# Node transposes moved behind the edge transposes and into the bank of the node sums

## The chip, the cores and the metric

One core of a Trainium2 chip runs the whole program. The metric is the device time of one execution in microseconds (us), as the median of several executions. Engines are named as in the profile: PE is TensorE's matmul, PEld its weight load, DVE is VectorE, ACT is ScalarE, POOL is GpSimd, SP is SyncE, which issues DMAs.

## What is computed

A graph layer over 50,000 nodes and 50,000 edges, 128 features each, in float32. `h` is the layer norm of `x` with negatives set to zero. Every edge takes its source's row of `h`, scales it by its weight, multiplies it with the 128x128 matrix of its type (one of 32) and is added to its destination. Every node also gets `h @ loop_weight + bias`. The matrices of the types are mixtures of 8 bases.

```python
h = jnp.maximum(_layernorm(x, axis=-1), 0.0)
W_rel = jnp.einsum('rb,bdf->rdf', w_comp, weight)
agg = jax.ops.segment_sum(h[src] * norm, seg, num_segments=n_rels * n_nodes)
node_repr = jnp.einsum('rnd,rdf->nf', agg.reshape(n_rels, n_nodes, d_in), W_rel)
out = x + jax.nn.relu(node_repr + h_bias + h @ loop_weight)
```

The edges come sorted by destination.

## The kernel before, in words

**Tiling.** Edges go in 98 groups (NG) of G = 4 tiles of 128 edges, nodes in 98 groups (NGW) of 4 windows of 128 nodes. One step `g` works on both at once, each part with its own lag, and there are 104 steps. Every engine has its own program, unrolled over the steps, in a hand-written order; engines meet only through semaphores. An engine takes its instructions strictly in order, so a wait holds up all that stands behind it.

**Edge side of step g.** POOL gathers rows of `x`. ACT subtracts means and applies relu (`normalised`, L685), PE transposes the four tiles of `h` into the PSUM bank `hT_ps` (L900), ACT copies the bank to `hT` (L719). In the next step PE multiplies each tile j with all eight bases: `messages(j)` is `product_high` (L813, bases 4 to 7) and `product_low` (L820, bases 0 to 3), each a 128x512 product which the trace shows as two matmul records. ACT scales three of the eight results (`scale_bases`: `z` L622 from the high product, then two `z` L626 from the low one), POOL adds two of them (`u` L526), and DVE adds the other five with the type's weights (L1075) and makes `msg` (L1108). I call DVE's block for one tile a slot: `tile_slot(j)`, which begins with the sum that reads the `z` of L622. Five PSUM banks `y_ps` take the products in rotation, so `product_high` of a tile waits until DVE has ended `sum_a` of three tiles before (L812), `product_low` until `sum_b` of two tiles before.

**Node side.** With lag 2 DVE takes statistics of `xw`. With lag 4 (RELU_AT) ACT makes `hw` for four windows (`window_relu`, L664, one after each of its four mixing blocks). With lag 5 (TURN_AT) PE transposes `hw` into `hT_ps` (`window_transposes`, L826), ACT copies that to `hwT` (`window_hT`, L673), and DVE makes the one-hot rows `pick` (`window_rows`, L1182). With lag 6 (SUMS_AT) PE multiplies `hwT` with the loop weight into the bank `win_ps` (`window_self`, L830), adds the messages to it with `pick` (`window_sums`, L835), and DVE reads the sums, applies relu and adds `x` (`window_results`, L1195). SP stores `res`.

**Order of PE in a step.** messages(0), messages(1), the node transposes of group g-5, the self products and sums of group g-6, messages(2), the small product for the type weights (L891), the four edge transposes, messages(3). Node and edge transposes share `hT_ps`, so the edge transposes wait for ACT's copy of the node ones (L898).

**Order of ACT in a step.** mixing(0), two normalised tiles, three square roots, window(0), mixing(1), two normalised tiles, the copy L673, window(1), mixing(2), the copy L719, window(2), two sums for means, mixing(3), two sums of squares, window(3).

**Order of DVE in a step.** slot 0, slot 1, the reciprocal and means, `window_rows`, `window_results`, slot 2, the type weights, slot 3, hot rows, shift and means of nodes. Each slot 0 and 1 ends with statistics of one edge tile and one window.

```python
messages(0)
messages(1)
if node_group(g, TURN_AT) is not None:
    window_transposes(g - TURN_AT)
...
pe.wait_ge(s_relu, g * G + G)
if node_group(g, TURN_AT) is not None:
    pe.wait_ge(n_hT_sb, g - TURN_AT + 1)
for j in range(G):
    mm = nc.tensor.transpose(hT_ps[:, j, :], h[:, q, j, :], ident[:, :])
mm.then_inc(s_hT, 1)
```

Of the kernel before, what the change touches and what calls it, by code (L numbers as in the profile page):

```python
# [20 lines left out]
ACT = mybir.ActivationFunctionType  # L21
# [17 lines left out]
HRING = 2  # L39
# [9 lines left out]
TURN_AT = 5  # L49
SUMS_AT = 6  # L50
# [29 lines left out]
def round_after(n, q, ring=RING):  # L80

    return n + (q + 1) // ring

def beyond(g, n):

    return isinstance(g, int) and g >= n

def is_before(g, n):  # L90

    return isinstance(g, int) and g < n
# [12 lines left out]
def build_layer(nc, x, src, dst_cols, dst, dst_next, type_rows, norm, dst_far, weight, mix_weight, loop_weight, bias, out):  # L105
    N, D = x.shape
    NT = src.shape[1]
    NG = NT // G
# [10 lines left out]
    STEPS = NGW + SUMS_AT  # L119
# [12 lines left out]
    with ctx:  # L132
        def sb(name, shape, dt=F32):
            return ctx.enter_context(nc.sbuf_tensor(name, shape, dt))

        def psum(name, shape, dt=F32):
            return ctx.enter_context(nc.psum_tensor(name, shape, dt))

        def sem(name):
            return ctx.enter_context(nc.semaphore(name))  # L140
# [6 lines left out]
        ident = sb("ident", [P, P])  # L147
# [75 lines left out]
        hw = sb("hw", [P, HRING, G, D])  # L223
        hwT = sb("hwT", [P, HRING, G, P])
# [16 lines left out]
        win_ps = psum("win_ps", [P, G, F])  # L241
        hT_ps = psum("hT_ps", [P, G, P])
# [8 lines left out]
        def late_bank(i):  # L251

            return y_ps[(2 * NG * G + i) % 5]

        def win_of(k):

            return win_ps if k < NGW - LATE else late_bank(k - (NGW - LATE))
# [25 lines left out]
        s_meta = sem("s_meta")  # L283
# [74 lines left out]
        n_hT_sb = sem("n_hT_sb")  # L358
        n_y = sem("n_y")
        n_res = sem("n_res")  # L360
# [6 lines left out]
        def node_group(g, at):  # L367

            return g - at if 0 <= g - at < NGW else None

        def windows_of(k):

            return G if k < NGW - 1 else LAST_FULL + 1
# [240 lines left out]
        def _(act):  # L614
# [54 lines left out]
            def window_hT(k):  # L669
                act.wait_ge(n_hT, k + 1)  # L670
                if k >= HRING:
                    act.wait_ge(n_y, k - (HRING - 1))
                nc.scalar.activation(hwT[:, k % HRING, :, :], hT_ps[:, :, :], ACT.Copy).then_inc(n_hT_sb, 1)  # L673

            def step(g, n, q):
                here = g < NG

                def mixing(j):
                    if 1 <= g <= NG:
                        scale_bases(g - 1, (q - 1) % RING, j)  # L680

                def normalised(tiles):

                    for j in tiles:
                        nc.scalar.activation(h[:, q, j, :], xg[:, q, j, :], ACT.Relu,  # L685
                                             bias=neg_mean[:, q, j:j + 1]).then_inc(s_relu, 1)

                def window(j):
                    k = node_group(g, RELU_AT)
                    if k is not None and j < windows_of(k):  # L690
                        window_relu(k, j)

                mixing(0)
                if here:
                    act.wait_ge(s_mean, g + 1)
                    act.wait_ge(s_squares, g * (G - DV))
                    if not is_before(g, RING):
                        act.wait_ge(s_hT, g - (RING - 1))
                    normalised(range(0, G // 2))
                    if not is_before(g, RING):  # L700
                        act.wait_ge(s_rstd, g - (RING - 1))
                    nc.scalar.activation(std[:, q, 0:DV], mv[:, q, :, 1], ACT.Sqrt, bias=eps_col[:, 0:1])
                    nc.scalar.activation(std[:, q, DV:G], squares[:, q, :], ACT.Sqrt, bias=eps_col[:, 0:1],
                                         scale=1.0 / D).then_inc(s_std, 1)
                if node_group(g, STD_AT) is not None:
                    window_std(g - STD_AT)
                window(0)
                mixing(1)
                if here:
                    normalised(range(G // 2, G))  # L710
                if node_group(g, TURN_AT) is not None:
                    window_hT(g - TURN_AT)
                window(1)
                mixing(2)
                if here:
                    act.wait_ge(s_hT, g + 1)
                    if not is_before(g, RING):
                        act.wait_ge(s_y, g * G - (RING - 1) * G)
                    nc.scalar.activation(hT[:, q, :, :], hT_ps[:, :, :], ACT.Copy).then_inc(s_hT_sb, 1)  # L719
                window(2)  # L720
                if not beyond(g, NG - 1):
                    group_means(g + 1, round_after(n, q), (q + 1) % RING)
                mixing(3)
                if not beyond(g, NG - 1):
                    group_squares(g + 1, (q + 1) % RING)
                window(3)
# [43 lines left out]

            first_step()
            sweep(act, STEPS, step, first=2)

            act.wait_ge(s_table, 16)
# [17 lines left out]
        def _(pe):  # L792
# [29 lines left out]

            def window_transposes(k):
                pe.wait_ge(n_h, k + 1)
                for j in range(windows_of(k)):
                    mm = nc.tensor.transpose(hT_ps[:, j, :], hw[:, k % HRING, j, :], ident[:, :])  # L826
                mm.then_inc(n_hT, 1)

            def self_loop(bank, v, j):
# [32 lines left out]
            def step(g, n, q):  # L862
                def messages(j):
                    if 1 <= g <= NG and not (is_before(g, 2) and j < PAIR):
                        if j == (PAIR if is_before(g, 2) else 0):
                            pe.wait_ge(s_hT_sb, g)
                        product_high(g - 1, (q - 1) % RING, j)
                        product_low(g - 1, (q - 1) % RING, j)

                messages(0)  # L870
                messages(1)
                if node_group(g, TURN_AT) is not None:
                    window_transposes(g - TURN_AT)
                if node_group(g, SUMS_AT) is not None:
                    for j in range(G):
                        window_self(g - SUMS_AT, j)
                if node_group(g, SUMS_AT) is not None and g != STEPS - 2:
                    if g == STEPS - 1:
                        window_sums(NGW - 2)
                    window_sums(g - SUMS_AT)  # L880
                messages(2)
                if is_before(g, 2):
                    messages(3)
                if g < NG:
                    pe.wait_ge(s_hot, g + 1)
                    if not is_before(g, 1):
                        pe.wait_ge(s_mix, g)
                    if g == CROWD_STEP:
                        pe.wait_ge(s_crowded, 1)
                        nc.tensor.matmul(mix_ps[0:1, 0:1], ones16[:, :], crowded16[:, :], start=True, stop=True)  # L890
                    nc.tensor.matmul(mix_ps[:, P:P + G * B], hotT[:, q, :], w_mix[:, :],  # L891
                                     start=True, stop=True).then_inc(s_mix_ps, 1)
                    if is_before(g, 1):
                        first_tiles()
                        return
                    pe.wait_ge(s_relu, g * G + G)
                    if node_group(g, TURN_AT) is not None:
                        pe.wait_ge(n_hT_sb, g - TURN_AT + 1)  # L898
                    for j in range(G):
                        mm = nc.tensor.transpose(hT_ps[:, j, :], h[:, q, j, :], ident[:, :])  # L900
                    mm.then_inc(s_hT, 1)
                if not is_before(g, 2):
                    messages(3)

# [23 lines left out]
            with pe.If(compact > 0):  # L928
# [8 lines left out]
                with pe.Fori(0, NGW) as g:  # L937
                    pe.wait_ge(f_h, g + 1)
                    hold(pe, passed["pe"])
                    for j in range(G):  # L940
                        mm = nc.tensor.transpose(hT_ps[:, j, :], hw[:, 0, j, :], ident[:, :])
# [10 lines left out]
        def _(dve):  # L952
# [245 lines left out]
            def window_results(k):  # L1198
                r = k % NRING
                dve.wait_ge(n_y, k + 1)  # L1200
                if k >= NRING:
                    dve.wait_ge(n_out[r], 16 * (k // NRING))
                results(win_of(k), r, k % XRING, windows_of(k)).then_inc(n_res, 1)

            def step(g, n, q):
                more, here = not beyond(g, NG - 1), not beyond(g, NG)
# [16 lines left out]
                    means(g + 1, (q + 1) % RING)  # L1223
                if g == STEPS - 3:
                    window_results(g - SUMS_AT)
                if node_group(g, TURN_AT) is not None:
                    window_rows(g - TURN_AT)
                if node_group(g, SUMS_AT) is not None and g != STEPS - 3:
                    window_results(g - SUMS_AT)
                tile_slot(g, n, q, 2, False)  # L1230
                stats_of(2)
# [205 lines left out]
```

## Time and profile before

| what | value |
|---|---|
| median of 3 runs | 1015.7 us (1014.95 to 1016.97) |
| the profiled execution, its own time | 1014.06 us |
| its span, first to last instruction | 1012.3 us |
| busy: PE, DVE, ACT, POOL | 995.7, 946.5, 882.8, 723.9 us |
| mean granted clock of TensorE | 0.995 of full speed |
| DMA | 154.46 MB, 153 GB/s mean |

A timeline lists instructions of one engine in order of time: start in us from the span's start, duration, engine, line, operation, tiles written and read, shape, count of merged instructions, and in brackets the idle time before and who ended it. Records of one engine overlap, since its instructions are pipelined, so the time that an instruction takes of its engine is read from start to start, not from its duration. The waits view gives the total, the number and the longest.

### The profile page before, as it was taken

Reading aid. Unit: us, or ns where it says so; the run is one execution under the profiler, and the core shown is the slowest. Engines: PE = TensorE matmul, PEld = TensorE weight load, DVE = VectorE, ACT = ScalarE, POOL = GpSimd, SP = SyncE. Lnnn points to the kernel's source line nnn. Section 1 sums busy time; section 2 is a strip of 40 time slices with the busy share of each in tenths; the row PEclk is TensorE's granted clock in tenths of the full one; section 3 lists DMA queues with packets and bytes.
Section 4 is the critical chain, followed back from the end, with each engine's and each line's share of the span. In section 5 each row is a group of like instructions: output and inputs, shape, how many; then the busy total and the mean of one; then the engine's idle time right before and its main releaser. Section 6 shows DMA issues by size and latency. Waiting matters only on the chain.

```text
span 1012.3 us, 23603 instructions
## 1 busy us (share of the span) xinstructions
PE 995.7 (98%) x4912; PEld 578.3 (57%) x4912; DVE 946.5 (94%) x4372; ACT 882.8 (87%) x3237; POOL 723.9 (72%) x1183
## 2 busy tenths in 40 slices
PE   7999999999999999999999999999999999999996
PEld 3455655555656565655555555556565555565655
DVE  8899999999999999999999999999999999999995
ACT  6798988889898989898989898989888888989884
POOL 7887767777777777777777777777776777777740
PEclk9999999999999999999999999999999999999999
DMA  4556556555556565565565565565655655655544
GB/s 116 148 143 169 154 145 167 147 156 158 151 147 176 137 164 158 152 164 158 138 175 139 157 162 155 147 170 148 165 155 141 173 141 157 158 159 139 154 124 138
DMA packets 178222, 154.46 MB, mean 153 GB/s; under 512 B 17781, under 2 KB 151213, under 8 KB 178077
## 3 DMA queue, kind: packets, MB, share of 16 engines
q1 hardware_dynamic: 157261, 101.40, 36.0%
q0 software_dynamic: 20384, 51.32, 20.7%
q14 instruction: 105, 0.86, 0.3%
q8 instruction: 40, 0.66, 0.3%
q10 hardware_dynamic: 432, 0.22, 0.1%
HBM read 101.31 MB, written 51.56 MB: 151 GB/s over the span
## 4 chain that ended last, share of the span: by engine, by line
PE 95%; ACT 2%; DVE 1%; POOL 1%; DMA 1%; issue 1%; ACTq 0%; DVEq 0%; POOLq 0%
PE y_ps L813 34%; PE y_ps L820 32%; PE win_ps L835 9%; PE win_ps L830 8%; PE hT_ps L900 4%; PE hT_ps L826 4%; PE mix_ps L891 1%; POOL xg L573 0%; DMA xg<-x,src_all 0%; ACT z L626 0%; ACT hw L664 0%; PE y_ps L835 0%; DMA src_all<-src 0%; PE y_ps L830 0%; DVE sum_a L1075 0%
## 5 line engine op out<-in xcount | busy, mean ns | idle before, releaser
L573 POOL DMA_INDIRECT xg<-x,src_all x392 | 386.6, 986 | 65.1 <-issue 48.6
L813 PE MATMUL y_ps<-w_all,hT 128*128 128x512 f32 x784 | 412.9, 608 | 3.3 <-DVE sum_a L1075 2.2
L820 PE MATMUL y_ps<-w_all,hT 128*128 128x512 f32 x784 | 401.9, 594 | 0.0
L526 POOL TENSOR_TENSOR u<-z 128x128 f32<-128x128 f32 x392 | 180.9, 461 | 189.5 <-ACT z L626 186.0
L626 ACT ACTIVATE z<-y_ps,mix 128x128 f32<-128x128 f32 x784 | 244.8, 367 | 45.3 <-PE y_ps L820 45.2
L1075 DVE SCALAR_TENSOR_TENSOR sum_b<-y_ps,mix,sum_b 128x128 f32<-128x128 f32 x784 | 266.4, 340 | 0.1
L820 PEld LDWEIGHTS y_ps<-w_all,hT 128*128 128x128 f32 x784 | 149.5, 191 | 188.6 <-issue 148.3
L813 PEld LDWEIGHTS y_ps<-w_all,hT 128*128 128x128 f32 x784 | 133.2, 190 | 118.0 <-DVE sum_a L1075 61.3
L622 ACT ACTIVATE z<-y_ps,mix 128x128 f32<-128x128 f32 x392 | 141.0, 360 | 62.6 <-PE y_ps L813 61.6
L664 ACT ACTIVATE hw<-xw,shift,nrstd 128x128 f32<-128x128 f32 x391 | 192.8, 494 | 0.4 <-DVE shift L1177 0.4
L1075 DVE SCALAR_TENSOR_TENSOR sum_b<-y_ps,mix,z 128x128 f32<-128x128 f32 x392 | 133.1, 339 | 47.7 <-ACT z L622 47.4
L1075 DVE SCALAR_TENSOR_TENSOR sum_a<-y_ps,mix,u 128x128 f32<-128x128 f32 x392 | 133.8, 341 | 2.9 <-POOL u L526 2.9
L685 ACT ACTIVATE h<-xg,neg_mean 128x128 f32<-128x128 f32 x384 | 135.1, 413 | 0.0
L1075 DVE SCALAR_TENSOR_TENSOR sum_a<-y_ps,mix,sum_a 128x128 f32<-128x128 f32 x392 | 134.0, 342 | 0.3 <-DVE sum_b L1075 0.2
L1108 DVE TENSOR_TENSOR msg<-sum_a,sum_b 128x128 f32<-128x128 f32 x392 | 113.7, 290 | 0.1
L1160 DVE BATCH_NORM_STATS2 nstats<-xw 128x6 f32<-128x128 f32 x391 | 106.9, 274 | 0.0
L835 PE MATMUL win_ps<-seg,pick 105*64 105x128 f32 x1504 | 103.0, 278 | 0.0
L830 PE MATMUL win_ps<-w_loop,hwT 128*128 128x128 f32 x752 | 99.3, 275 | 0.0
L830 PEld LDWEIGHTS win_ps<-w_loop,hwT 128*128 128x128 f32 x752 | 91.4, 192 | 0.0
L835 PEld LDWEIGHTS win_ps<-seg,pick 105*64 105x64 f32 x1504 | 80.2, 136 | 11.3
L559 POOL DMA_DIRECT2D xw<-x x97 | 78.0, 805 | 6.9 <-issue 6.9
L826 PEld LDWEIGHTS hT_ps<-ident,hw 128*128 128x128 f32 x391 | 48.6, 141 | 53.6 <-issue 49.7
(124 smaller groups left out, 1166.1 us busy)
## 6 DMA issues: line engine op xcount, KB each, us to landing
seg<-msgs SPq DMA_DIRECT2D x391, 104.8 KB
msgs<-msg SPq DMA_DIRECT2D x98, 258.0 KB, 2.7
xw<-x POOLq DMA_DIRECT2D x97, 256.0 KB
out<-res SPq DMA_DIRECT2D x97, 256.0 KB, 3.1
xg<-x,src_all POOLq DMA_INDIRECT x392, 3.4
type_bc<-type_rows SPq DMA_DIRECT2D x52, 112.0 KB
w_all<-weight SPq DMA_DIRECT2D x1, 512.0 KB, 4.0
type_bc<-type_rows SPq DMA_DIRECT2D x4, 80.0 KB
```

The costliest lines, as they stand in the source:

```text
L526: nc.gpsimd.tensor_tensor(u[:, r, :], z[:, r, 0, :], z[:, r, 1, :], ALU.add).then_inc(s_u, 1)
L573: nc.gpsimd.indirect_dma_start(xg[:, q, j, :], None, x, bass.IndirectOffsetOnAxis(ap=src_all[:, g * G + j:g * G + j + 1], axis=0)).then_in ...
L622: nc.scalar.activation(z[:, r, 2, :], product(t, B // 2), ACT.Copy, scale=mix[:, q, j, B // 2:B // 2 + 1]).then_inc(s_z_high, 1)
L626: ins = nc.scalar.activation(z[:, r, b, :], product(t, b), ACT.Copy, scale=mix[:, q, j, b:b + 1])
L664: ins = nc.scalar.activation(hw[:, v, j, :], xw[:, q, j, :], ACT.Relu, bias=shift[:, r, j:j + 1], scale=nrstd[:, r, j:j + 1])
L685: nc.scalar.activation(h[:, q, j, :], xg[:, q, j, :], ACT.Relu, bias=neg_mean[:, q, j:j + 1]).then_inc(s_relu, 1)
L813: nc.tensor.matmul(y_ps[2 * t % 5][:, :, :], hT[:, q, j, :], w_all[:, B // 2:B, :], start=True, stop=True).then_inc(s_y_high, 1)
L820: nc.tensor.matmul(y_ps[(2 * t + 1) % 5][:, :, :], hT[:, q, j, :], w_all[:, 0:B // 2, :], start=True, stop=True).then_inc(s_y, 1)
L830: nc.tensor.matmul(bank[:, j, :], hwT[:, v, j, :], w_loop[:, :], start=j == 0, stop=False)
L835: mm = nc.tensor.matmul(bank[:, j, :][c * HALF:(c + 1) * HALF], pick[:, v, j, c, :][0:SEG_P + 1], seg[0:SEG_P + 1, q, j, c, 0:F], start=Fa ...
L1075: return nc.vector.scalar_tensor_tensor(out=acc, in0=product(t, base), scalar=c[:, base:base + 1], in1=first, op0=ALU.mult, op1=ALU.add)
L1108: nc.vector.tensor_tensor(msg[:, q, j, 0:F], sum_a[:, r, :], sum_b[:, r, :], ALU.add).then_inc(s_msg, 1)
```

## The change

In the steps up to 97 (`g < NG`) the node transposes of group g-5 move from between messages(1) and the self products to directly behind the four edge transposes, ahead of messages(3). They write `win_ps`, the bank of the node sums, and no longer `hT_ps`. For this they wait until DVE has read the sums of group g-6 from that bank (`n_res`), in the same step. The edge transposes no longer wait for ACT's copy of the node transposes. ACT makes that copy (L673) behind mixing(3) and no longer ahead of window(1). DVE does `window_results` ahead of `window_rows`. From step 98 on everything is as before.

```diff
+        def turned(k):
+
+            return win_ps if k + TURN_AT < NG else hT_ps
...
-                nc.scalar.activation(hwT[:, k % HRING, :, :], hT_ps[:, :, :], ACT.Copy).then_inc(n_hT_sb, 1)
+                nc.scalar.activation(hwT[:, k % HRING, :, :], turned(k)[:, :, :], ACT.Copy).then_inc(n_hT_sb, 1)
...
                 if here:
                     normalised(range(G // 2, G))
-                if node_group(g, TURN_AT) is not None:
+                if node_group(g, TURN_AT) is not None and not here:
                     window_hT(g - TURN_AT)
                 window(1)
...
                 mixing(3)
+                if node_group(g, TURN_AT) is not None and here:
+                    window_hT(g - TURN_AT)
                 if not beyond(g, NG - 1):
                     group_squares(g + 1, (q + 1) % RING)
...
             def window_transposes(k):
                 pe.wait_ge(n_h, k + 1)
+                if turned(k) is win_ps:
+                    if k == 0:
+                        pe.wait_ge(s_meta, 1)
+                    else:
+                        pe.wait_ge(n_res, k)
                 for j in range(windows_of(k)):
-                    mm = nc.tensor.transpose(hT_ps[:, j, :], hw[:, k % HRING, j, :], ident[:, :])
+                    mm = nc.tensor.transpose(turned(k)[:, j, :], hw[:, k % HRING, j, :], ident[:, :])
                 mm.then_inc(n_hT, 1)
...
                 messages(1)
-                if node_group(g, TURN_AT) is not None:
+                if node_group(g, TURN_AT) is not None and g >= NG:
                     window_transposes(g - TURN_AT)
...
                     pe.wait_ge(s_relu, g * G + G)
-                    if node_group(g, TURN_AT) is not None:
-                        pe.wait_ge(n_hT_sb, g - TURN_AT + 1)
                     for j in range(G):
                         mm = nc.tensor.transpose(hT_ps[:, j, :], h[:, q, j, :], ident[:, :])
                     mm.then_inc(s_hT, 1)
+                    if node_group(g, TURN_AT) is not None:
+                        window_transposes(g - TURN_AT)
...
                     window_results(g - SUMS_AT)
+                if node_group(g, SUMS_AT) is not None and g < NG:
+                    window_results(g - SUMS_AT)
                 if node_group(g, TURN_AT) is not None:
                     window_rows(g - TURN_AT)
-                if node_group(g, SUMS_AT) is not None and g != STEPS - 3:
+                if node_group(g, SUMS_AT) is not None and g >= NG and g != STEPS - 3:
                     window_results(g - SUMS_AT)
```

## Rows read from the trace of the kernel before

**Rows 1.** The page: busy us, share of the span and instructions of each engine
```profile
PE 995.7 (98%) x4912; PEld 578.3 (57%) x4912; DVE 946.5 (94%) x4372; ACT 882.8 (87%) x3237; POOL 723.9 (72%) x1183
```

**Rows 2.** The page: the chain that ended last, share of the span by engine
```profile
PE 95%; ACT 2%; DVE 1%; POOL 1%; DMA 1%; issue 1%; ACTq 0%; DVEq 0%; POOLq 0%
```

**Rows 3.** The same chain in order of time: start, us, what
```profile
105.69 1.05 PE y_ps L813 x2
...
988.92 1.07 PE y_ps L813 x2
```

**Rows 4.** Timeline of PE, step 52 and the start of step 53
```profile
524.87 0.60 PE L826 MATMUL hT_ps<-ident,hw 128*128 128x128 f32 x4
525.30 1.06 PE L830 MATMUL win_ps<-w_loop,hwT 128*128 128x128 f32 x8
...
529.28 0.63 PE L900 MATMUL hT_ps<-ident,h 128*128 128x128 f32 x4
529.75 1.02 PE L813 MATMUL y_ps<-w_all,hT 128*128 128x512 f32 x2
530.61 1.02 PE L820 MATMUL y_ps<-w_all,hT 128*128 128x512 f32 x2
...
534.90 0.60 PE L826 MATMUL hT_ps<-ident,hw 128*128 128x128 f32 x4
```

**Rows 5.** Timeline of ACT, step 52 and the start of step 53
```profile
526.91 0.61 ACT L673 ACTIVATE hwT<-hT_ps 128x512 f32<-128x512 f32 x1
527.39 0.51 ACT L664 ACTIVATE hw<-xw,shift,nrstd 128x128 f32<-128x128 f32 x1
...
529.95 0.60 ACT L719 ACTIVATE hT<-hT_ps 128x512 f32<-128x512 f32 x1
...
531.67 0.63 ACT L626 ACTIVATE z<-y_ps,mix 128x128 f32<-128x128 f32 x2
...
533.34 0.35 ACT L622 ACTIVATE z<-y_ps,mix 128x128 f32<-128x128 f32 x1
...
535.61 0.37 ACT L622 ACTIVATE z<-y_ps,mix 128x128 f32<-128x128 f32 x1
```

**Rows 6.** Timeline of DVE, step 52 and slots 0 and 1 of step 53
```profile
530.03 0.35 DVE L1075 SCALAR_TENSOR_TENSOR sum_a<-y_ps,mix,sum_a 128x128 f32<-128x128 f32 x1
...
531.79 0.35 DVE L1075 SCALAR_TENSOR_TENSOR sum_b<-y_ps,mix,z 128x128 f32<-128x128 f32 x1 [0.58 <-ACT z L622]
...
534.04 0.32 DVE L1075 SCALAR_TENSOR_TENSOR sum_b<-y_ps,mix,z 128x128 f32<-128x128 f32 x1
...
536.01 0.35 DVE L1075 SCALAR_TENSOR_TENSOR sum_b<-y_ps,mix,z 128x128 f32<-128x128 f32 x1
...
538.09 0.69 DVE L1182 TENSOR_TENSOR pick<-iota_n,rel 104x512 f32<-104x512 f32 x1
538.69 0.69 DVE L1195 SCALAR_TENSOR_TENSOR res<-win_ps,xw 128x512 f32<-128x512 f32 x1
```

**Rows 7.** Timeline of all engines, step 5: the only edge transposes that waited for L673
```profile
56.30 0.60 ACT L673 ACTIVATE hwT<-hT_ps 128x512 f32<-128x512 f32 x1
...
57.01 0.42 PEld L900 LDWEIGHTS hT_ps<-ident,h 128*128 128x128 f32 x4 [0.24 <-issue]
...
57.04 0.63 PE L900 MATMUL hT_ps<-ident,h 128*128 128x128 f32 x4 [0.16 <-ACT hwT L673]
...
57.51 1.02 PE L813 MATMUL y_ps<-w_all,hT 128*128 128x512 f32 x2
```

**Rows 8.** Timeline of PEld, first weight load of step 52's node transposes
```profile
524.44 0.14 PEld L826 LDWEIGHTS hT_ps<-ident,hw 128*128 128x128 f32 x1 [0.24 <-issue]
```

**Rows 9.** L1108 alone: ns min/median/max, first and last start; timeline of DVE, step 63
```profile
L1108 DVE TENSOR_TENSOR msg<-sum_a,sum_b x392: 268/282/498, 17.7 to 995.3; 128x128 f32<-128x128 f32 x196
...
637.83 0.47 DVE L1108 TENSOR_TENSOR msg<-sum_a,sum_b 128x128 f32<-128x128 f32 x1
```

**Rows 10.** Timeline of POOL, step 53: the sum that slot 1 reads
```profile
535.13 0.47 POOL L526 TENSOR_TENSOR u<-z 128x128 f32<-128x128 f32 x1
```

## The prediction

> **What bounds the kernel now.** I read the page first: PE is busy for 995.7 of 1012.3 us, DVE for 94%, ACT for 87% [rows 1], and 95% of the chain that ended last is PE [rows 2]. A busy PE need not be one without stalls, so I went on to the chain in order of time. The same L813 comes back at 105.69 and, 88 steps later, at 988.92 [rows 3]: 883.23 / 88 = 10.04 us a step, and the timeline of steps 52 and 53 shows 534.90 - 524.87 = 10.03 [rows 4]. PE has no gap in it. So PE sets the pace with its own instructions, and a change can gain only by making PE's list shorter, and loses whatever it makes PE wait. What matters next is how close the other engines' results come to the moment at which PE needs them.
>
> **PE's own list.** Nothing is added or removed: four transposes go from one place to another. At the old place they take 525.30 - 524.87 = 0.43 us from start to start, or 0.11 each [rows 4]. At the new place they stand behind four others of the same form that take 529.75 - 529.28 = 0.47 to the next product [rows 4], 0.03 of which is a first one that is longer. Eight in a row I put at 0.47 + 4 x 0.11 = 0.91 against 0.43 + 0.47 = 0.90 now. Where the self products now stand directly behind a product, I know no row for that switch; between a gain of the 0.03 and a loss of the same I take 0. So PE's demand stays at 10.03 us, and undisturbed messages(3) of step 53 still starts at 529.75 + 10.03 = 539.78.
>
> **Waits removed.** The edge transposes lose their wait for ACT's copy of the node ones. It held PE once, in step 5 [rows 7]: the transposes came 0.16 us behind the last matmul's recorded end. As small matmuls follow each other at 0.11 where they overlap, I count 0.3 us gained. From step 6 on the wait costs nothing, as PE has no gap.
>
> **Waits added and moved.** The node transposes now wait for DVE's `res` of the same step. The question is whether it is there in time. I follow a ring, step 52 to 53.
>
> 1. PE ends the low product of messages(3) at 530.61 + 1.02 = 531.63, and ACT's `z` of it starts at 531.67 [rows 4, 5]. In the new order the edge transposes come 0.44 earlier in the step, so the copy L719 and what follows it start 0.44 earlier, but this `z` can't, since messages(3) stays where it was. ACT waits there, and the time it won is lost. This is the step on which the forecast hangs.
> 2. Behind this `z` stands the moved copy L673. It takes ACT 527.39 - 526.91 = 0.48 us [rows 5]. From 531.67 to the `z` of 535.61, which slot 1 of step 53 reads, ACT goes from instruction to instruction without idle time [rows 5]. So that `z` goes from 535.61 to 536.09, and its end from 535.98 to 536.46. (Before, L673 stood behind it, and had cover: ACT waits for PE ahead of mixing(2).)
> 3. DVE's slot 1 starts 0.03 behind the end of that `z`: 536.01 against 535.98 [rows 5, 6]. It is held by it, in nearly every step. So slot 1 starts at 536.49.
> 4. From there to the first of the two large operations DVE takes 538.09 - 536.01 = 2.08 us [rows 6]. In the new order that first one is `res`: start 538.57, end 538.57 + 0.69 = 539.26. Without the swap with `pick` it would be 0.60 later (538.69 - 538.09), so the swap is needed and is not enough.
> 5. PE's hop behind another engine's result: in step 5 the copy ended at 56.90, the weight load came at 57.01, the matmul at 57.04, and messages(3) at 57.51 [rows 7]. That is 0.11 + 0.03 + 0.47. With it the node transposes start at 539.40 and messages(3) at 539.87, against 539.78 undisturbed. PE loses 0.09 us, and as everything in the ring hangs on messages(3), it loses that in each step: the period goes from 10.03 to 10.12.
>
> The hop has no row for this place, so I bound it. Below, a hop of 0.04, as ACT's behind PE (531.63 to 531.67): the load at 539.30 and the matmul at 539.33, where 529.75 - 0.44 + 10.03 = 539.34 was due; no loss. Above, a whole weight load of 0.11 exposed in place of the 0.03: 539.37 + 0.11 + 0.44 = 539.92, so 0.14 lost. I take 0.09, from the row of the same instruction with the same kind of wait.
>
> **What the rest costs.** DVE's slot 0 of step 53 begins at 534.04 while the `z` for it, at 533.34, ends at 533.69 [rows 5, 6]; 0.48 later that is 534.17, so slot 0 starts at 534.20, 0.16 later, which slot 1's new start covers. Slot 3 had 0.58 us of idle time ahead of it [rows 6]; it takes up that slot 2 is 0.48 later. POOL's `u` for slot 1 starts at 535.13 [rows 10], behind a gather and not behind ACT: no change. The swap makes `pick` 0.69 later; it is read a whole step later. No DMA is issued at another place of its queue; those of `res` become due at nearly the same time. Steps from 98 on are as before.
>
> **Long `msg`.** L1108 takes 282 ns, at times up to 498 [rows 9]: in step 63 0.47 in place of 0.28. I found one in slot 1 (or a gap of that size ahead of `pick`) in every seventh step from 49 to 91 and in some four before. PE never felt it, since DVE stood idle later. Now it lies in the ring: 11 x 0.19 = 2.1 us.
>
> **The sum.** The wait is there in steps 6 to 97: 92 x 0.09 = 8.3; long `msg` 2.1; step 5 -0.3. Together +10.1 us. The profiled execution took 1014.06 us, so 1024.2; it lies 1.6 under the median of 1015.7, which then goes to 1025.8.
>
> **A rule that speaks otherwise.** In step 5 the weight load itself stood behind the wait, 57.01 after 56.90, while without a wait it runs one matmul ahead: 524.44 for a matmul at 524.87 [rows 7, 8]. The Trainium skill, "TensorE: Matmul & The Clock Gate", the table at its head, says that PE has a queue of 64 with a partial reorder window that pulls weight loads ahead of matmuls in flight. By that rule the first load of the node transposes could be done before the wait ends, and the sum would be that of the second rival.
>
> **Rivals.**
> - *The ring closes without loss (same).* The first weight load is done ahead, or the hop is 0.04. Then the transposes start at 539.30 to 539.34, in time, and only the long `msg` show, some of them in part: +0.5 to +2, 1016.2 to 1017.7. For it: only 0.09 separates the two. Against it: step 5, where the wait held the load.
> - *Faster.* PE's list gets shorter: the moved transposes no longer interrupt the way from product to self product, and the chain of small ones pays one long first instruction less, at most 0.03 a step. If also the ring closes: 92 x 0.03 = 2.8 less, 1012.9. It decides as soon as `res` ends by 539.17. Against: each 0.01 of it has to come from one switch, and step 4 above leaves `res` at 539.26.
> - *A second wait joins (slower still).* Slot 2 starts 0.48 later too. The `sum_a` of it, at 530.03, ends at 530.38, so at 530.86 then; `product_high` of the next messages(0) waits for it. That product is due at 530.61 + 0.86 = 531.47 and its load a matmul's time (0.43) ahead, 531.04 [rows 4, 6, 8]. With the hop of 0.11 the load can go at 530.97: 0.07 to spare. If slot 2 slips by over 0.07 more (a later `z` or `u`), the matmul waits; with 0.1 a step on top of the 0.09: 92 x 0.19 + 2.1 = 19.6, 1035. Against: it has the full 0.07, and what PE loses ahead of messages(3) is added to it.
>
> **How the numbers follow.** Forecast 0.68, no loss 0.14, faster 0.04, second wait 0.14. About 0.2%, 2 us, is what a measurement can tell here. Slower by more: 0.68 + 0.14, and a little of the third, 0.83; within: 0.13; faster: 0.04. The forecast's own bounds are 0.02 to 0.14 a step, 1.8 + 1 to 12.9 + 2.1 us, so 1018.5 to 1030.7; another 0.02 to 0.03 a step for DVE's first read of a bank by `res` where `pick` read none gives up to 1033. The range is 1017.5 to 1033.
>
> **What would show it.** Right: `PE hT_ps L900` no longer among the waits; the node transposes (L826, now writing `win_ps`) waiting for `DVE res L1195` with gaps around 0.1 in every step; step period 10.12 in the chain; `z` L626 of mixing(3) behind some 0.4 of idle time on ACT; slot 1 still 0.03 behind its `z`. Wrong: a period of 10.03 and no such wait (the load went ahead or ACT's later part has slack that I don't see); waits of L813 for `sum_a`; a PE list that is shorter or longer between the same two instructions.

## The result, and the profile after

| | before | after |
|---|---|---|
| median | 1015.7 us (1014.95 to 1016.97, 5 runs) | 1024.5 us (1024.31 to 1025.66, 5 runs) |
| profiled execution, own time | 1014.06 us | 1024.31 us |
| span | 1012.3 us | 1022.4 us |
| PE busy | 995.7 us | 1004.9 us |

The ratio is 1.0086, with a 95% interval of 1.0075 to 1.0097: slower by 8.8 us. The forecast for the median was 1025.8, with a range of 1017.5 to 1033.

**The page does not show the loss as idle time.** Here are its busy line and the chain's shares by engine, which answer to [rows 1, 2]:

```profile
PE 1004.9 (98%) x4912; PEld 580.8 (57%) x4912; DVE 950.3 (93%) x4372; ACT 893.1 (87%) x3237; POOL 719.6 (70%) x1183
...
PE 80%; DVE 11%; ACT 4%; issue 3%; POOL 1%; another core or an unknown queue 0%; ACTq 0%; DVEq 0%; POOLq 0%
```

PE is as busy as before, 98%, and its busy time has grown by 9.2 us with the same 4912 instructions. The chain tells more: some of it now runs over DVE and ACT. The groups of PE show the same (last column: idle time ahead of the group, and who ended it):

```profile
L819 PE MATMUL y_ps<-w_all,hT 128*128 128x512 f32 x784 | 413.2, 609 | 5.1 <-DVE sum_a L1086 3.6 <-ACT hT L773 1.0 <-issue 0.5
...
L837 PE MATMUL win_ps<-ident,hw 128*128 128x128 f32 x372 | 58.3, 279 | 0.2 <-DVE res L1206 0.2
```

The node transposes (L837 now) have 0.2 us of idle time charged to `res` in the whole run, all of it in one step (31). The record of the last edge transpose is 0.27 us long while its successor could start after 0.11, so a wait of 0.1 hides inside it. It has to be read from start to start, in the timeline of PE (steps 51 to 52 of this kernel; start, duration):

```profile
525.44 0.63 PE L909 MATMUL hT_ps<-ident,h 128*128 128x128 f32 x4
525.98 0.63 PE L837 MATMUL win_ps<-ident,hw 128*128 128x128 f32 x4
526.45 1.02 PE L819 MATMUL y_ps<-w_all,hT 128*128 128x512 f32 x2
527.31 1.02 PE L826 MATMUL y_ps<-w_all,hT 128*128 128x512 f32 x2
...
535.57 0.63 PE L909 MATMUL hT_ps<-ident,h 128*128 128x128 f32 x4
536.11 0.63 PE L837 MATMUL win_ps<-ident,hw 128*128 128x128 f32 x4
536.58 1.02 PE L819 MATMUL y_ps<-w_all,hT 128*128 128x512 f32 x2
```

with, in the timeline of all engines, the weight load of the node transposes at 536.11:

```profile
536.08 0.42 PEld L837 LDWEIGHTS win_ps<-ident,hw 128*128 128x128 f32 x4
```

From the edge transposes to the node ones it is 0.54 us and from there 0.47 to messages(3): 1.01 for the eight, where I had counted 0.91. From one messages(3) to the next, 536.58 - 526.45 = 10.13 us against 10.03 in [rows 4].

Over the whole stretch in which the wait stands, from messages(3) of step 5 to that of step 97, the two timelines of PE give, with 57.51 [rows 7] as the start before (first the end before, then start and end after):

```profile
981.25 1.02 PE L813 MATMUL y_ps<-w_all,hT 128*128 128x512 f32 x2
...
59.80 1.02 PE L819 MATMUL y_ps<-w_all,hT 128*128 128x512 f32 x2
...
992.27 1.02 PE L819 MATMUL y_ps<-w_all,hT 128*128 128x512 f32 x2
```

That is 923.74 us before and 932.47 after, or 10.041 and 10.136 for each of the 92 steps: 8.7 us more, which is the 8.8 of the medians.

ACT in the same stretch, which answers to [rows 5]:

```profile
527.58 0.36 ACT L626 ACTIVATE z<-y_ps,mix 128x128 f32<-128x128 f32 x1
528.37 0.63 ACT L630 ACTIVATE z<-y_ps,mix 128x128 f32<-128x128 f32 x2 [0.43 <-PE y_ps L826]
528.88 0.60 ACT L677 ACTIVATE hwT<-win_ps 128x512 f32<-128x512 f32 x1
529.36 0.41 ACT L652 ACTIVATE h<-xg,neg_mean 128x128 f32<-128x128 f32 x1
...
532.79 0.37 ACT L626 ACTIVATE z<-y_ps,mix 128x128 f32<-128x128 f32 x1
```

and DVE, where the first row answers to [rows 6]:

```profile
533.20 0.35 DVE L1086 SCALAR_TENSOR_TENSOR sum_b<-y_ps,mix,z 128x128 f32<-128x128 f32 x1 [0.24 <-ACT z L626]
...
535.28 0.69 DVE L1206 SCALAR_TENSOR_TENSOR res<-win_ps,xw 128x512 f32<-128x512 f32 x1
```

The whole ring can be read off: messages(3) starts at 526.45; its low product ends at 527.31 + 1.02 = 528.33; the `z` starts at 528.37, behind the 0.43 us of idle time that the forecast spoke of; the `z` of slot 1 starts at 532.79, that is 4.42 later, where it was 535.61 - 531.67 = 3.94 [rows 5]; it ends at 533.16 and slot 1 starts at 533.20; `res` starts 2.08 later, at 535.28, and ends at 535.97; the weight load of the node transposes comes at 536.08, 0.11 later, and the first transpose at 536.11, 0.14 later; messages(3) 0.47 after that, at 536.58. Every piece has the size that the forecast gave it, within 0.01 us.

### The profile page after: what moved, and what is told of

The parts are those of the page before. It is cut to its first block, busy times and chain, and to the rows that moved or that the text cites. A ratio compares the mean times of both kernels' runs of the same rounds, so it can differ in the third digit from the quotient of the medians.

```text
span 1022.4 us, 23603 instructions
## 1 busy us (share of the span) xinstructions
PE 1004.9 (98%) x4912; PEld 580.8 (57%) x4912; DVE 950.3 (93%) x4372; ACT 893.1 (87%) x3237; POOL 719.6 (70%) x1183
## 4 chain that ended last, share of the span: by engine, by line
PE 80%; DVE 11%; ACT 4%; issue 3%; POOL 1%; another core or an unknown queue 0%; ACTq 0%; DVEq 0%; POOLq 0%
PE y_ps L819 29%; PE y_ps L826 27%; PE win_ps L846 8%; PE win_ps L841 7%; PE win_ps L837 4%; PE hT_ps L909 4%; DVE sum_a L1086 3%; DVE sum_b L1086 3%; ACT h L652 1%; PE mix_ps L902 1%; DVE pick L1193 1%; DVE msg L1119 1%; DVE nstats L1171 1%; ACT hw L668 1%; ACT z L626 1%
## 5 line engine op out<-in xcount | busy, mean ns | idle before, releaser
L530 POOL TENSOR_TENSOR u<-z 128x128 f32<-128x128 f32 x392 | 189.3, 483 | 205.2 <-ACT z L630 187.9
L630 ACT ACTIVATE z<-y_ps,mix 128x128 f32<-128x128 f32 x784 | 246.9, 371 | 83.5 <-PE y_ps L826 47.6
L626 ACT ACTIVATE z<-y_ps,mix 128x128 f32<-128x128 f32 x392 | 143.1, 365 | 23.7 <-PE y_ps L819 19.0
L689 ACT ACTIVATE h<-xg,neg_mean 128x128 f32<-128x128 f32 x384 | 136.3, 419 | 0.0
L841 PEld LDWEIGHTS win_ps<-w_loop,hwT 128*128 128x128 f32 x752 | 98.6, 192 | 44.0 <-issue 44.0
L1119 DVE TENSOR_TENSOR msg<-sum_a,sum_b 128x128 f32<-128x128 f32 x392 | 111.3, 284 | 0.1
L652 ACT ACTIVATE h<-xg,neg_mean 128x128 f32<-128x128 f32 x194 | 76.5, 406 | 0.0
```

Of the source, the lines that this page charges most:

```text
L530: nc.gpsimd.tensor_tensor(u[:, r, :], z[:, r, 0, :], z[:, r, 1, :], ALU.add).then_inc(s_u, 1)
L626: nc.scalar.activation(z[:, r, 2, :], product(t, B // 2), ACT.Copy, scale=mix[:, q, j, B // 2:B // 2 + 1]).then_inc(s_z_high, 1)
L630: ins = nc.scalar.activation(z[:, r, b, :], product(t, b), ACT.Copy, scale=mix[:, q, j, b:b + 1])
L841: nc.tensor.matmul(bank[:, j, :], hwT[:, v, j, :], w_loop[:, :], start=j == 0, stop=False)
L1119: nc.vector.tensor_tensor(msg[:, q, j, 0:F], sum_a[:, r, :], sum_b[:, r, :], ALU.add).then_inc(s_msg, 1)
```

## The experiments

All edits are made to the changed kernel. A step's mean length is taken from the view of the node transposes alone, as (last start - first start - 0.3) / 92, since 92 steps lie between the two and the last start is that of the fourth transpose of its group. That view's row, one from each kernel's trace, the changed kernel first:

```profile
L837 PE MATMUL win_ps<-ident,hw x372: 272/273/302, 59.4 to 992.2; 128*128 128x128 f32 x186
```

(992.2 - 59.4 - 0.3) / 92 = 10.136.

### 1. The copy ahead of mixing(3)

```diff
-                mixing(3)
                 if node_group(g, TURN_AT) is not None and here:
                     window_hT(g - TURN_AT)
+                mixing(3)
```

> The changed kernel with ACT's copy of the node transposes directly ahead of mixing(3) in place of directly behind it. Theory (the ring: the copy's 0.48 us lie between the z of messages(3) and DVE's slot 1, and so make res late): ACT has 0.43 us idle ahead of the second z of mixing(3), the copy now fills that, the z starts at most 0.05 later, res ends 0.43 to 0.48 earlier, the node transposes no longer wait, the period falls from 10.13 to 10.03 to 10.04 and the time to 1015 to 1016. Rival A (TensorE's own list is longer with eight transposes in a row in two banks): ACT's order changes nothing, 1024.5, period 10.13. Rival B (the wait for res costs its hop whenever it stands there, early or late): no change either, 1024.5, and gaps ahead of the node transposes stay.

Measured: 1015.9 us, ratio to the kernel before 1.0002 (0.9993 to 1.0011). One block of ACT's order takes away all of the loss that the medians can show. Mean step from the row

```profile
L837 PE MATMUL win_ps<-ident,hw x372: 272/273/302, 59.4 to 984.0; 128*128 128x128 f32 x186
```

is 10.047, against 10.041 before. What is left lies in a few steps from 21 to 45, behind those in which DVE checks the edges' order besides: step 42, the longest of them, takes 10.31 in place of 10.03. In the timeline of its PE nothing stands between the two groups of transposes:

```profile
531.90 0.63 PE L909 MATMUL hT_ps<-ident,h 128*128 128x128 f32 x4
532.37 0.60 PE L837 MATMUL win_ps<-ident,hw 128*128 128x128 f32 x4
532.81 1.02 PE L819 MATMUL y_ps<-w_all,hT 128*128 128x512 f32 x2
```

0.47 + 0.44 = 0.91 for all eight. And in the timeline of its ACT the copy fills the idle time:

```profile
534.03 0.58 ACT L677 ACTIVATE hwT<-win_ps 128x512 f32<-128x512 f32 x1
534.51 0.36 ACT L626 ACTIVATE z<-y_ps,mix 128x128 f32<-128x128 f32 x1
534.76 0.62 ACT L630 ACTIVATE z<-y_ps,mix 128x128 f32<-128x128 f32 x2
```

The product that this `z` reads starts at 533.67 and ends at 534.69, so the `z` at 534.76 starts 0.07 behind that end, where the changed kernel's starts 0.04 behind it. Rival A (PE's own list is longer) and rival B (the wait costs wherever it stands) are out: both the eight transposes and the wait are still there.

### 2. Another piece of ACT ahead of mixing(3)

```diff
+                if here:
+                    window(3)
                 mixing(3)
...
-                window(3)
+                if not here:
+                    window(3)
```

> The changed kernel with window(3), the fourth relu of the node side (0.38 us of ACT, nobody waits for it early), ahead of mixing(3) in place of behind it; the copy stays behind mixing(3). Theory (any ACT work between the z of messages(3) and the z of slot 1 counts, whichever it is): that stretch becomes 0.38 shorter, res ends 0.38 earlier, over four times the 0.09 that is lost; period 10.03, 1015 to 1016, the same as with the copy moved. Rival (it is the copy itself, as the only reader of the bank with the node transposes, that matters): it still stands behind mixing(3), so 1024.5.

Measured: 1015.2 us, ratio 0.9999 (0.9990 to 1.0009). The copy stayed behind mixing(3) and the loss is gone all the same. What matters is how much of ACT's work lies between the two `z`, not which. Step: (982.4 - 58.2 - 0.3) / 92 = 10.042, from

```profile
L840 PE MATMUL win_ps<-ident,hw x372: 272/273/302, 58.2 to 982.4; 128*128 128x128 f32 x186
```

### 3. The wait on the weight load

```diff
-                pe.wait_ge(n_h, k + 1)
-                if turned(k) is win_ps:
-                    if k == 0:
-                        pe.wait_ge(s_meta, 1)
-                    else:
-                        pe.wait_ge(n_res, k)
+                if turned(k) is win_ps and k > 0:
+                    pe.wait_ge(n_res, k)
+                pe.wait_ge(n_h, k + 1)
+                if k == 0:
+                    pe.wait_ge(s_meta, 1)
```

 Theory of the hop (the 0.14 us from the end of res to the first node transpose are in part the sequencer standing at the wait with nothing sent on): the wait on the weight load itself takes about what ACT shows behind PE, 0.04, plus 0.03 to the matmul, so 0.07 in place of 0.14; period 10.06, 1017.5 to 1019. Rival (the hop is the same in either form, or the load that waits is then exposed in full): 1024.5 plus or minus 2.

Measured: 1018.2 us, ratio 1.0027 (1.0018 to 1.0037). The same two waits in the other order are worth 6.3 us. The timeline of all engines shows the hop:

```profile
530.64 0.68 DVE L1205 SCALAR_TENSOR_TENSOR res<-win_ps,xw 128x512 f32<-128x512 f32 x1
...
531.38 0.42 PEld L836 LDWEIGHTS win_ps<-ident,hw 128*128 128x128 f32 x4
531.40 0.63 PE L836 MATMUL win_ps<-ident,hw 128*128 128x128 f32 x4
...
531.87 0.59 PE L819 MATMUL y_ps<-w_all,hT 128*128 128x512 f32 x1
```

`res` ends at 531.32; 0.06 to the load and 0.08 to the matmul, against 0.14 before. The mean step is (984.7 - 57.5 - 0.3) / 92 = 10.075, 0.06 shorter:

```profile
L836 PE MATMUL win_ps<-ident,hw x372: 272/273/330, 57.5 to 984.7; 128*128 128x128 f32 x186
```

0.06 x 92 = 5.6. Time and period came out as the theory had them (1017.5 to 1019, 10.06), so the order of the two waits matters. That the wait written second is an instruction of its own is the theory's account of it; no row shows such an instruction. Even so the load did not go ahead of the wait.

### 4. DVE's swap undone

```diff
-                if node_group(g, SUMS_AT) is not None and g < NG:
-                    window_results(g - SUMS_AT)
                 if node_group(g, TURN_AT) is not None:
                     window_rows(g - TURN_AT)
+                if node_group(g, SUMS_AT) is not None and g < NG:
+                    window_results(g - SUMS_AT)
```

> The changed kernel with DVE's swap undone: one-hot rows first, then the results, as in the kernel before. Theory (res lies in the ring, and every 0.1 us by which it is later is 0.1 a step): res is 0.60 later, period 10.73, 92 steps x 0.60 = 55, so 1078 to 1081. Rival (res lay only just behind what TensorE needs and other work gives way when it is later, as slot 2 and P0's wait for sum_a take over): clearly less than 40 us more, under 1065.

Measured: 1079.2 us, ratio 1.0627 (1.0610 to 1.0643). The whole 0.60 is paid in every step: (1047.8 - 60.3 - 0.3) / 92 = 10.730, 0.59 above the changed kernel. So the ring is closed, and no other wait takes a share of it. Here the wait is long enough to show as idle time, in the view of the same stretch:

```profile
531.88 0.68 DVE L1206 SCALAR_TENSOR_TENSOR res<-win_ps,xw 128x512 f32<-128x512 f32 x1
...
532.71 0.63 PE L837 MATMUL win_ps<-ident,hw 128*128 128x128 f32 x4 [0.51 <-DVE res L1206]
```

The hop is 532.71 - 532.56 = 0.15 again. The step's length is from

```profile
L837 PE MATMUL win_ps<-ident,hw x372: 272/273/302, 60.3 to 1047.8; 128*128 128x128 f32 x186
```

### 5 and 6. One more square root, behind the copy or ahead of mixing(3)

```diff
                     window_hT(g - TURN_AT)
+                    nc.scalar.activation(root[:, :], eps_col[:, :], ACT.Sqrt)
```

> The changed kernel with one more square root of a column on ACT directly behind the copy, in steps 5 to 97; nobody reads it. A square root takes ACT 0.19 us from start to start. Theory (the ring has no slack at all, so each unit of ACT's time in that stretch is a unit of every step): period 10.13 + 0.19 = 10.32, 92 x 0.19 = 17 on top, so 1041 to 1043. Rival (ACT or DVE have slack further on that takes part of it): clearly under 1038.

```diff
+                if node_group(g, TURN_AT) is not None and here:
+                    nc.scalar.activation(root[:, :], eps_col[:, :], ACT.Sqrt)
                 mixing(3)
```

> The same square root, but directly ahead of mixing(3), where ACT in the changed kernel has 0.43 us idle before the second z. Theory: no change against the changed kernel, 1024 to 1025, period 10.13. Rival (it is ACT's total work that counts, 87% busy and near its limit): as much as behind the copy, about 1042.

Measured: behind the copy 1032.8 us, ratio 1.0180 (1.0164 to 1.0195); ahead of mixing(3) 1023.7 us, ratio 1.0088 (1.0073 to 1.0104), the changed kernel's own.

The first missed its number, and by its words the rival (slack further on) would have it. The trace says otherwise. In the timeline of ACT the root took half of what I had put:

```profile
531.37 0.60 ACT L677 ACTIVATE hwT<-win_ps 128x512 f32<-128x512 f32 x1
531.84 0.21 ACT L730 ACTIVATE root<-eps_col 128x1 f32<-128x1 f32 x1
531.93 0.41 ACT L652 ACTIVATE h<-xg,neg_mean 128x128 f32<-128x128 f32 x1
```

531.93 - 531.84 = 0.09 us from start to start. I had taken 0.19 from the kernel's own square roots, which read a bias tile; the added one has none. The mean step is

```profile
L838 PE MATMUL win_ps<-ident,hw x372: 272/273/302, 57.9 to 998.8; 128*128 128x128 f32 x186
```

(998.8 - 57.9 - 0.3) / 92 = 10.224, which is 0.09 above 10.136. So the ring took all of the cost, and the size of the cost was wrong. The same work ahead of mixing(3) left the mean step at (990.7 - 58.0 - 0.3) / 92 = 10.135:

```profile
L839 PE MATMUL win_ps<-ident,hw x372: 272/273/302, 58.0 to 990.7; 128*128 128x128 f32 x186
```

The amount of ACT's work does not count here, its place does.

### 7. Copy ahead, and the swap undone

The edits of 1 and 4 together.

> The changed kernel with both: the copy ahead of mixing(3), and DVE's one-hot rows ahead of the results as before. Theory: res then ends where it did in the kernel before, 539.38 on the clock of its step 53; 0.14 to the first node transpose and 0.47 to messages(3) give 539.99 against 539.78, so 0.21 a step, 92 x 0.21 = 19, 1034 to 1036. So the swap is worth only 0.2 here where it is worth 0.6 with the copy behind. Rival (additive: undoing the swap costs 0.60 a step whatever the rest): 1070.

Measured: 1039.1 us, ratio 1.0235 (1.0220 to 1.0251). It is far from additive, as expected, but 3 us over the upper end of the forecast, 1036. Two pieces can be told apart: most steps are 10.25 long, as forecast (10.24), and some are longer. One of these is step 63; in the timeline of all engines:

```profile
654.65 0.46 POOL L530 TENSOR_TENSOR u<-z 128x128 f32<-128x128 f32 x1
654.80 0.47 DVE L1119 TENSOR_TENSOR msg<-sum_a,sum_b 128x128 f32<-128x128 f32 x1
...
657.01 0.63 PE L837 MATMUL win_ps<-ident,hw 128*128 128x128 f32 x4 [0.21 <-DVE res L1206]
```

This is the long `msg` of [rows 9]. It stands in slot 1 in steps 14, 28, 35, 49, 56, 63, 70, 77, 84 and 91, and each of these steps is about 0.18 longer than its neighbours: 1.8 us. Most of the rest lies in steps 21 to 45, where DVE has checks of the edges' order to do besides. That these checks are the cause was not tried by itself.

### 8. Copy ahead, and the wait on the weight load

The edits of 1 and 3 together.

> The changed kernel with the copy ahead of mixing(3) and the wait for res on the first weight load (its sequence of waits swapped). Theory: TensorE's own list is the bound again and nothing is left to win, period 10.03, 1015 to 1016, no difference from the kernel before that can be measured; the steps in which DVE's added checks of the order of edges lie (20 to 44, every third) lose less than with the copy ahead alone. Rival (the eight transposes in a row, no longer waiting, make TensorE's list shorter by up to 0.03 a step): 1012.5 to 1013.5.

Measured: 1015.7 us, ratio 1.0008 (0.9999 to 1.0017). PE's list bounds the kernel again, and it is no shorter. The steps behind DVE's checks lose less than in experiment 1, as expected: step 42 takes 10.25 in place of 10.31. The experiments point to no version that beats the kernel before: they only take away what was added.

## Why the prediction was right

**Where PE stands.** "PE has no gap in it", and a change loses whatever it makes PE wait: right. In experiments 1, 2 and 8, where the wait reaches PE in a few steps only, the time is that of the kernel before.

**PE's own list.** I put eight transposes at 0.91 and the switch from product to self product at 0. Experiment 1 measured 0.47 + 0.44 = 0.91 and a time that can't be told from before. The rival that PE's list gets shorter is out with it.

**The ring.** All five of its pieces came out within 0.01 us: the `z` of mixing(3) held by messages(3), 0.48 of the copy, 0.03 to slot 1, 2.08 to `res`, 0.14 + 0.47 to messages(3). Experiments 1 and 2 shorten it at ACT, 3 at the hop, 4 at DVE, and 5 lengthens it; each changed the step by what it took or gave, and the same work outside of it (6) changed nothing.

**The hop.** I took 0.11 + 0.03 from the one place of the kernel before where the same kind of instruction stood at the same kind of wait, and between bounds of 0 and 0.14 lost per step that gave 0.09. Measured 0.10 at the start-to-start distances in most steps, 0.095 in the mean. What I had not seen is that this number belongs to the order of the two waits: experiment 3 has 0.08 in all. In the kernel before, too, the edge transposes have two waits and the late one, for ACT's copy, is written second, so the row had the right form; that it did was luck. The 0.02 to 0.03 that the range allows for DVE's first read of a bank had no row, and nothing of it came: slot 1 to the large operation is 2.08 in both kernels.

**The rule on weight loads that run ahead.** Sum by the row: a loss of 0.09 a step; by the Trainium skill's rule ("TensorE: Matmul & The Clock Gate", the table at its head), no loss. The time decides for the row in this place. The first weight load of the node transposes starts only behind the end of `res`, 0.11 behind it in the changed kernel and 0.06 in experiment 3. The page says only that loads are pulled ahead of matmuls in flight; that they pass a wait was my reading of it, and no run here shows that.

**The second wait.** It did not join. PE's idle time charged to `sum_a` is 3.6 us against 2.2 before, but all of it lies ahead of 49 us, before the first step that the change touches. Even in experiment 4 the cost was the 0.60 alone.

**The signs.** The forecast looked for gaps of about 0.1 ahead of the node transposes in every step, charged to `res`. The wait is there, but the view of idle time does not show it, since it hides in the record of the transpose before it; of the signs named, the period, the idle time of ACT and slot 1 close behind its `z` are the ones that showed.

**What was off.** The term for long `msg`, 2.1 us, and the 0.3 gained in step 5. From messages(3) of step 4 to that of step 6 it is 18.83 us before and 18.85 after, so nothing was gained there. In the changed kernel's trace slot 1 has no long `msg` from step 14 to 91. The same view as [rows 9]:

```profile
L1119 DVE TENSOR_TENSOR msg<-sum_a,sum_b x392: 270/280/536, 18.7 to 1006.3; 128x128 f32<-128x128 f32 x196
```

shows that some are still there (536 ns), but they lie elsewhere. I had carried a row of the old trace over to the new one as if it belonged to the step, while it belongs to the meeting of two engines at that moment, and the change moved slot 1 by 0.48 us and most of POOL's sums less. With the ring alone the sum is 92 x 0.095 = 8.7 at the measured mean, or 8.3 at my 0.09; measured 8.8. The profiled executions differ by 10.25, 1.4 more. Messages(3) of step 5 comes 2.29 us later in the changed kernel's trace than in the one before (59.80 against 57.51). The code up to step 4 is the same in all the changed kernels, and yet their node transposes of step 5 start anywhere from 57.4 to 60.3 us; so a difference of one profiled execution against another carries some 2 us of the start, and the medians are the better measure.

## What to carry to other kernels

Where one engine runs without a gap, read for every wait that a change adds the moment at which that engine gets there and the moment at which the releaser is done, and follow the releaser back until the ring meets the bound engine again; in these runs work inside such a ring cost its full length in every step and work just outside of it cost nothing. When a step has to move on a second engine, put it ahead of the place where that engine waits for the bound one, not behind it. Of two waits ahead of a weight load, write the late one first; here that was worth 6.3 us.

## What the runs showed of the hardware that was not expected

- **Two prices of a square root on ACT.** The added one-column square root took 0.09 us from start to start in experiment 5. In the same trace the kernel's own three, of two, two and four columns, take 0.19, 0.18 and 0.19, the first two ahead of another square root, the last ahead of a relu. All three read a bias tile and the added one reads none. The rows point to the bias tile rather than to the columns or the neighbour, but no run varied it alone.

```profile
534.61 0.30 ACT L707 ACTIVATE std<-squares,eps_col 128x2 f32<-128x2 f32 x1
534.79 0.30 ACT L660 ACTIVATE nstd<-nmv,eps_col 128x4 f32<-128x4 f32 x1
534.98 0.50 ACT L668 ACTIVATE hw<-xw,shift,nrstd 128x128 f32<-128x128 f32 x1
```

- **A DVE add that starts early inside a POOL add ends late.** The kernel before, timeline, step 56:

```profile
567.43 0.46 POOL L526 TENSOR_TENSOR u<-z 128x128 f32<-128x128 f32 x1
567.60 0.45 DVE L1108 TENSOR_TENSOR msg<-sum_a,sum_b 128x128 f32<-128x128 f32 x1
...
570.86 0.28 DVE L1108 TENSOR_TENSOR msg<-sum_a,sum_b 128x128 f32<-128x128 f32 x1
```

  The `msg` that starts 0.17 us behind the start of a POOL add ends 0.16 behind its end, and takes 0.45; the next, alone, takes 0.28. In this trace 16 of 17 `msg` over 0.4 us start within 0.2 us behind the start of such an add. In experiment 4 it is 95 of 96. Another 67 `msg` of the kernel before start 0.35 us or more behind the start of such an add, still inside it, and take 0.27 to 0.29. The Trainium skill, "GPSIMD Engine Reference", section 1, says that POOL shares its SBUF interfaces with VectorE and contends with VectorE instructions that have two SBUF inputs; `msg` is one, and the rows agree. That this is the cause was not tried by an experiment of its own.
